# Graph attention of one Trainium2 core: the edge terms built feature by edge instead of edge by feature, and the scores summed in PSUM

## The reference

```python
for i in range(3):
    gl = (h @ Wl[i] + bl[i]).reshape(n, 4, 32)
    gr = (h @ Wr[i] + br[i]).reshape(n, 4, 32)
    xj = gl[src]                                  # a row per edge
    e = xj + gr[dst] + (edge_attr @ We[i])        # edge x 4 heads x 32
    e = leaky_relu(e, 0.2)
    alpha = einsum('ehc,hc->eh', e, att_w[i])     # 4 scores of an edge
    alpha = exp(alpha - segment_max(alpha, dst)[dst])
    alpha = alpha / (segment_sum(alpha, dst)[dst] + 1e-16)
    h = segment_sum(xj * alpha[..., None], dst) + bias[i]
    h = leaky_relu(batch_norm(h, gamma[i], beta[i]), 0.02)
out = h @ Wf + bf
```

## Time and profile before

| | |
|---|---|
| time, median of 3 | 6846.17 us (6832.88 to 6849.38) |
| the profiled execution's time | 6835.19 us |
| its span | 6833.4 us |
| busy: PE, DVE, ACT, POOL | 5228.6, 4419.9, 2485.9, 4656.5 us |
| attention, first gather to last | 3469.4 to 4485.0, 4586.5 to 5601.8, 5705.4 to 6724.0 us |

### The profile page before, as it was taken

The page is one execution under the profiler, slowest core; times in us unless marked ns, Lnnn a source line. Parts: engine busy times, 40 slices in busy tenths (PEclk is TensorE's granted clock), DMA queues, the critical chain, the costliest instruction groups (busy, mean ns, idle before and its releaser), DMA issues.

```text
span 6833.4 us, 117887 instructions
## 1 busy us (share of the span) xinstructions
PE 5228.6 (77%) x33433; PEld 4525.5 (66%) x33433; DVE 4419.9 (65%) x15206; ACT 2485.9 (36%) x9471; POOL 4656.5 (68%) x4868
## 2 busy tenths in 40 slices
PE   8988851888888788788667777767777776777776
PEld 7555541777777677777556666656666665666675
DVE  5434330777676788877757777765766774777776
ACT  2554420777776587777501111110111111111112
POOL 1777776777776477777357777737777764777772
PEclk9999985999999899999879999978999997989887
DMA  2111111544444355544134444434444443444442
GB/s 65 41 39 39 42 24 57 131 126 126 126 126 112 94 151 151 147 142 142 52 108 136 140 135 132 138 79 129 136 140 133 131 121 93 136 135 135 132 132 68
DMA packets 496381, 755.03 MB, mean 110 GB/s; under 512 B 226141, under 2 KB 358593, under 8 KB 494709
## 3 DMA queue, kind: packets, MB, share of 16 engines
q1 hardware_dynamic: 314500, 425.53, 19.9%
q0 software_dynamic: 180928, 315.57, 19.4%
q10 hardware_dynamic: 320, 6.40, 0.4%
HBM read 647.92 MB, written 98.34 MB: 109 GB/s over the span
## 4 chain that ended last, share of the span: by engine, by line
POOL 20%; PE 15%; DVE 13%; issue 11%; DMA 4%; DVEq 2%; ACT 1%; POOLq 0%; ACTq 0%
POOL AR L577 13%; POOL AR L569 7%; PE PS L1342 5%; DVE AR L1938 4%; PE PS L1358 4%; PE PS L1355 3%; DMA AR<-gtab_d,AR 3%; DVE AR L2007 2%; DVE AR L2018 1%; DVEq L505 1%; DMA AR<-ptab_d,AR 1%; PE PS L1256 1%; PE PS L1232 1%; PE PS L1253 1%; DVE AR L2028 1%
## 5 line engine op out<-in xcount | busy, mean ns | idle before, releaser
L577 POOL DMA_INDIRECT AR<-gtab_d,AR x2436 | 2310.8, 949 | 848.2 <-issue 702.1
L569 POOL DMA_INDIRECT AR<-ptab_d,AR x1624 | 1546.7, 952 | 529.1 <-issue 476.7
L1358 PE MATMUL PS<-AR,ident 128*128 128x140 f32 x4872 | 1115.5, 313 | 246.2 <-DMA AR<-gtab_d,AR 243.0
L1342 PE MATMUL PS<-AR 128*112 128x132 f32 x4872 | 895.5, 318 | 395.8 <-DVE AR L1938 368.7
L1355 PE MATMUL PS<-AR 128*128 x4872 | 1093.5, 309 | 68.1 <-issue 67.9
L1342 PEld LDWEIGHTS PS<-AR 128*112 128x112 f32 x4872 | 704.3, 200 | 542.2 <-DVE AR L1938 259.0
L1358 PEld LDWEIGHTS PS<-AR,ident 128*128 128x128 f32 x4872 | 846.8, 212 | 311.2 <-DMA AR<-gtab_d,AR 309.5
L551 POOL DMA_INDIRECT rec_d<-AR x782 | 771.3, 986 | 371.0 <-issue 235.3
L1023 ACT ACTIVATE AR<-AR 128x448 f32<-128x448 bf16 x609 | 335.3, 570 | 1776.2 <-PE PS L1342 1598.5
L2018 DVE SCALAR_TENSOR_TENSOR AR<-PS,AR 128x280 f32<-128x280 f32 x1218 | 536.9, 445 | 674.9 <-PE PS L1358 672.6
L1256 PE MATMUL PS<-AR,ident 128*128 128x160 f32 x3248 | 790.3, 325 | 223.1 <-DMA AR<-ptab_d,AR 218.3
(11 more groups left out here) (347 smaller groups left out, 7417.4 us busy)
## 6 DMA issues: line engine op xcount, KB each, us to landing
AR<-ste_d SPq DMA_DIRECT2D x404, 512.0 KB
AR<-nbb_d SPq DMA_DIRECT2D x303, 224.0 KB
ste_d<-AR SPq DMA_DIRECT2D x101, 512.0 KB
AR<-gtab_d,AR POOLq DMA_INDIRECT x2436
AR<-ptab_d,AR POOLq DMA_INDIRECT x1624
nbb_d<-AR SPq DMA_DIRECT2D x101, 224.0 KB, 2.4
AR<-key_d SPq DMA_DIRECT2D x94, 224.0 KB
AR<-rec_d SPq DMA_DIRECT2D x812, 8.0 KB
```

Of the source, the lines that this page charges most:

```text
L569: e.indirect_dma_start(out=XJ1[:, t % 32, :], out_offset=None, in_=tabs_d[0][:, :], in_offset=off).then_inc(done_, 16)
L577: e.indirect_dma_start(out=xj2(t)[:, t % 4, :], out_offset=None, in_=tabs_d[1][:, :], in_offset=off).then_inc(done_, 16)
L1342: x = e.matmul(PS[6 + v_ % 2][0:B, (t % 2) * 132:(t % 2 + 1) * 132], SQ4[:, i % 4, t % 4, :], PX[:, i % 5, t % 4, :, :].rearrange("p h c - ...
L1358: x = e.matmul(o, ident[:, :], xj2(t)[:, t % 4, :], start=False, stop=True, skip_group_check=True)
```

## The change

The edge terms of a tile are built turned over. PE transposes the gathered rows (`e.transpose`, 128 columns) into PSUM and adds the product of the right table's block with `STE`, so that features lie along the partitions and edges along the columns. ACT copies each tile's block of the right table into a fixed place first (`expander`, a ring `EX` of 12), since it is now the stationary operand of the product. A quad fills one PSUM bank (128 x 512). ACT takes it out with the bias (`LE`), DVE does the leaky ReLU on it within SBUF (`leaked`), and PE makes the scores: a product with a window of `ATW`, a matrix that holds the attention vectors, the window shifted by one column for every tile, so that all tiles of a chunk accumulate in one bank, already in the form that the scans want. The extra columns of the left table, `terms`, `scores`, `AL` and its turning are gone. A row of the table is 132 wide instead of 140 (`GW`), features are kept in another order, the right table is taken out of PSUM by ACT instead of DVE (`gat_out`), with two banks in turn for each table instead of four shared ones, and the products that made the extra columns of the weights are gone.

The rounds change too: chunks of eight quads up to quad 184 (before up to 152), then four of 6, 5, 4 and 4 quads, 27 in all instead of 29 (`NCH`), a chunk's steps in successive rounds throughout (before two rounds apart in 17 chunks), and one quad weighted in each round, 12 rounds after its own (before two in every second round, with 17 to 9 rounds between). The ring `XJ` is 32 quads long instead of 29. `LASTR` is 217 instead of 214.

```diff
-HW = 35
+HW = 33
 GW = 4 * HW
-NXJ = 29
+NXJ = 32
@@ rounds_of_attention
-    ends = list(range(8, 153, 8)) + list(range(157, 198, 5)) + [NQ]
+    ends = list(range(8, 185, 8)) + [190, 195, 199, NQ]
...
-        gap = 2 if c < 17 else 1
-        turn = end + gap
+        turn = end + 1
...
-        back = max(turn + 2 * gap + 1 + gap, px[-1] + 1 if px else 0)
-        steps.append((turn, turn + gap, turn + 2 * gap, turn + 2 * gap + gap - 1, back))
-        for i in range(start, end):
-            r = max(back + 2 - gap, px[-1] if px else 0)
-            while px.count(r) >= 2:
-                r += 1
-            px.append(r)
+        back = max(turn + 3, px[-1] + 1 if px else 0)
+        steps.append((turn, turn + 1, turn + 2, turn + 2, back))
+        px += [back + i for i in range(end - start)]
@@ scalar_program
+            def gat_out(l, b):
+                w.wait_ge(s_mm, mm_at(f"gat{l}", b))
+                done(e.activation(TABG[0:B, b, :], PS[6 + b % 2][0:B, 0:128], ACT.Copy), s_aev)
...
+                for j in range(-2, LASTR):
+                    if j + 2 < NQ:
+                        i = j + 2
+                        if i >= 3:
+                            w.wait_ge(s_e, pair_at(l, 2 * (i - 3) + 1))
+                        for t in range(4 * i, 4 * i + 4):
+                            x = e.activation(expander(t), TABG[:, bass.ds(block_of(cx, "scalar", t), 1), :].rearrange("p a f -> p (a f)"), ACT.Copy)
+                        done(x, s_ex)
...
+                    if 0 <= j < NQ:
+                        w.wait_ge(s_e, pair_at(l, 2 * j + 1))
+                        if j >= 2:
+                            w.wait_ge(s_lin, quad_at(l, j - 2))
+                        done(e.activation(LE[:, j % 2, :], PS[j % 2][:, :], ACT.Identity, bias=BRC[:, l % 2:l % 2 + 1]), s_le)
...
-                for g in range(7):
-                    done(e.activation(XT[:, g * TG:(g + 1) * TG], XT[:, g * TG:(g + 1) * TG], ACT.Identity,
-                                      scale=ST[:, 18:19], bias=ST[:, 19:20]), s_aff)
+                for g in range(9):
+                    if g < 7:
+                        done(e.activation(XT[:, g * TG:(g + 1) * TG], XT[:, g * TG:(g + 1) * TG], ACT.Identity,
+                                          scale=ST[:, 18:19], bias=ST[:, 19:20]), s_aff)
+                    if l < 2 and g >= 2:
+                        for b in range(4 * g - 8, 4 * g - 4):
+                            gat_out(l + 1, b)
@@ tensor_program
-                    w.wait_ge(s_dev, dev_at(p, b - 4, 1))
-                    e.matmul(PS[4 + b % 4][0:B, 0:GW], XT[:, b * B:(b + 1) * B], WLx, start=True, stop=True, skip_group_check=True)
-                    done(e.matmul(PS[4 + b % 4][0:B, GW:2 * GW], XT[:, b * B:(b + 1) * B], WRx, start=True, stop=True, skip_group_check=True), s_mm)
...
+                    w.wait_ge(s_dev, dev_at(p, b - 2))
+                    w.wait_ge(s_aev, aev_at(p, b - 2))
+                    e.matmul(PS[4 + b % 2][0:B, 0:128], XT[:, b * B:(b + 1) * B], WLx, start=True, stop=True, skip_group_check=True)
+                    done(e.matmul(PS[6 + b % 2][0:B, 0:128], XT[:, b * B:(b + 1) * B], WRx, start=True, stop=True, skip_group_check=True), s_mm)
...
-                        if u >= 4:
-                            w.wait_ge(s_att, pair_at(l, u - 4))
...
+                        if u % 2 == 0 and u >= 4:
+                            w.wait_ge(s_le, quad_at(l, u // 2 - 2))
+                        w.wait_ge(s_ex, quad_at(l, u // 2))
                         for t in (2 * u, 2 * u + 1):
-                            o = PS[u % 4][:, (t % 2) * GW:(t % 2 + 1) * GW]
+                            o = PS[(u // 2) % 2][:, (t % 4) * 128:(t % 4 + 1) * 128]
+                            w.wait_ge(*gath_sem(l + 2, t))
+                            e.transpose(o, xj2(t)[:, t % 4, 0:128], ident[:, :])
                             w.wait_ge(*ste_sem(l + 2, t))
-                            e.matmul(o, STE[:, ste_slot(l + 2, t), (t % 8) * 128:(t % 8 + 1) * 128],
-                                     TABG[:, bass.ds(block_of(cp, "tensor", t), 1), :], start=True, stop=False, skip_group_check=True)
-                            w.wait_ge(*gath_sem(l + 2, t))
-                            x = e.matmul(o, ident[:, :], xj2(t)[:, t % 4, :], start=False, stop=True, skip_group_check=True)
+                            x = e.matmul(o, expander(t), STE[:, ste_slot(l + 2, t), (t % 8) * 128:(t % 8 + 1) * 128],
+                                         start=False, stop=True, skip_group_check=True)
                         done(x, s_e)
...
+                    def scores(i):
+                        c = chunk_of(i)
+                        w.wait_ge(s_att, quad_at(l, i))
+                        w.wait_ge(s_arg, chunk_at(l, c - 2))
+                        for kk in range(4):
+                            t = 4 * (i - chunk_start(c)) + kk
+                            x = e.matmul(PS[2 + c % 2][:, 0:128], ATW[:, 31 - t:159 - t], LE[:, i % 2, kk * 128:(kk + 1) * 128],
+                                         start=(t == 0), stop=(i == ENDS[c] - 1 and kk == 3), skip_group_check=True)
+                        done(x, s_lin)
...
+                    if 1 <= j <= NQ:
+                        scores(j - 1)
@@ vector_program
-                    done(e.tensor_tensor(ZG[:, b, :], PS[4 + b % 4][0:B, 0:GW], BLb, ALU.add), s_dev)
-                    done(e.tensor_tensor(TABG[0:B, b, :], PS[4 + b % 4][0:B, GW:2 * GW], BRb, ALU.add), s_dev)
+                    done(e.tensor_tensor(ZG[:, b, 0:128], PS[4 + b % 2][0:B, 0:128], BLb[:, 0:128], ALU.add), s_dev)
...
-                def terms(u):
...
-                    done(e.scalar_tensor_tensor(
-                        AB[:, j % 2, kk:kk + 2, :], PS[u % 4][:, 0:2 * GW].rearrange("p (k f) -> p k f", k=2), 0.0,
-                        attB.unsqueeze(1).to_broadcast([128, 2, GW]), ALU.max, ALU.mult), s_att)
-                def scores(j):
...
-                    done(e.tensor_reduce(AL[:, c % 2, :, t0:t0 + 4].rearrange("p h t -> p t h"),
-                                         AB[:, j % 2, :, :].rearrange("p k (h c) -> p k h c", h=4), AX.X, ALU.add), s_lin)
+                def leaked(j):
+                    w.wait_ge(s_le, quad_at(l, j))
+                    done(e.scalar_tensor_tensor(LE[:, j % 2, :], LE[:, j % 2, :], 0.2, LE[:, j % 2, :], ALU.mult, ALU.max), s_att)
...
                     if j < NQ:
-                        terms(2 * j)
-                        add()
-                        terms(2 * j + 1)
-                        add()
-                        scores(j)
-                        add()
-                    if len(quads) > 1:
-                        add()
-                        weight(quads[1])
+                        leaked(j)
                     while tiles:
                         add()
```

More of the change, by code:

```diff
@@ L488, in groups_up_to @@
             return sum(1 for _, lo, _ in SG if load_of(lo) <= i)
-        ENG = {"vector": mybir.EngineType.DVE, "tensor": mybir.EngineType.PE}
+        ENG = {"vector": mybir.EngineType.DVE, "tensor": mybir.EngineType.PE, "scalar": mybir.EngineType.Activation}
         def record_tile(cache, t):
@@ L556, in gpsimd_program @@
                 w.wait_ge(s_dve, DV[("henc", "h0_3", "h1_3", "ov0_6", "ov1_6")[layer]])
-                mile(e.memset(acc_flat, 0.0), f"acc{layer}")
+                mile(e.memset(acc_flat if layer < 2 else acc2, 0.0), f"acc{layer}")
                 if layer < 2:
@@ L2062, in vector_program @@
                     quads = weighted_in(j)
+                    add()
+                    if quads:
+                        weight(quads[0])
+                    add()
                     for n, step in ((0, scans), (1, carries), (2, args)):
@@ L2155, in arrange @@
     h = lambda n: i["L1_gnn_" + n]
+    by_head = np.arange(128).reshape(4, 32).T.reshape(-1)
+    inner = lambda x: c(x[..., by_head])
+    layers = lambda x: c(np.stack([x[0], x[1][by_head], x[2][by_head]])[..., by_head])
     return {
```

171 lines of the change are left out of this document (72 added, 99 removed).

## The result

The changed kernel takes 6876.37 us (median of 5, 6867.27 to 6887.12) against 6846.17 (median of 5, 6832.88 to 6850.21): a ratio of 1.005, with a 95% interval of 1.0033 to 1.0067. The profiled executions have spans of 6874.2 and 6833.4 us, 40.8 apart.

What follows compares the result with a forecast made beforehand. POOL's issue of attention gathers was taken as the bound. Terms +60 (`leaked`), -1 (chunk steps), -52 (tails), -3 (ahead of layer one), +1 (projections) make +5 on 6846.17: 6851, stated as 6852, range 6791 to 6930.

Steps and rivals of the forecast that it cites:

- A: Attention layers: POOL stays the bound and `leaked` meets some gathers; 6814 to 6904 us, chance 0.52.
- POOL is the bound and stays it: Attention layers: POOL's gathers, 1.25 us apart, wait for nobody between a layer's first and last; 3 x 1015 us.
- `leaked` lengthens the gathers that start under it, by what is left of it less 0.13 us: Attention gathers: `leaked`, both inputs in SBUF, delays a gather's end by its remaining time less 0.13 us, 609 occurrences.
- The size of that term: Gathers lengthened by `leaked`: 0.121 us each at random phase, 74 us in all; 60 booked, bounds 0 and 300.
- a fixed part of the phases: Gathers meeting `leaked`: some phases always harmless, so 60 us taken instead of 74.
- The tails: Last gather to normalising step in each layer: 46 us instead of 62.6, 63.7 and 66.8; -52 us booked.
- in the tail a round costs what DVE and PE need: Rounds after a layer's last gathers: 3 x 0.45 + 0.82 = 2.2 us each, without `pair` and `leaked`; 40 us taken.
- case D: Tails don't shorten because PE and DVE wait for one another's answers: +57 us, 6903, chance 0.08.
- The loop under 5.0 us: PE, ACT and DVE loop per round: 4.1 us at full clock, 6.4 at half, mean 4.5, below POOL's 5.0.
- The lower price for the transpose: PE's transpose in the attention rounds: 0.11 to 0.22 us, between half a product and a whole one.
- Projections and the start of layer one: Projections +1 us over three layers from two banks; -3 us ahead of layer one, extra-column products gone.
- Case B: Attention layers: `leaked` locks into a harmless place behind a gather's start; -55 us, 6791, chance 0.25.

Runs made afterwards that it cites:

- e3: Kernel before plus, per quad ahead of the weighting, a product of gathered rows with themselves, both inputs in SBUF: 8803.13 us against 8492.64 on a slow chip.
- e4: Kernel before with the weighting done twice, one input in SBUF and one in PSUM: 8822.79 us against 8492.64 on a slow chip.
- e9: Changed kernel with the leaky ReLU's maximum taken from PSUM, one input in SBUF: 6789.83 us against 6842.49 of the kernel before, ratio 0.9926.
- e10: Changed kernel with the maximum from PSUM and a layer's last 19 quads weighted two in a round: 6791.11 us, 0.992 of the kernel before.

## Why the prediction was right, point by point

It said 6852 with a range of 6791 to 6930; measured were 6876.37. The signs of the terms and the case were right (A, own range 6814 to 6904), the point 24 us too low. Between the two profiles the sum was +5 and came out as +40.8: of the 35.8 between, 14.6 lie in the layers, 13.4 in the tails, 6.9 in the first part, mostly the one long transfer. That `leaked` was the price and the tails the gain was no luck; but the two large terms nearly cancel, both were set too favourably, and the range, 139 us wide, held either sign.

- **POOL is the bound and stays it**: shown. Idle time before the gathers is 848.2 and 848.9 us; of it 702.1 and 733.9 are issue, 107 in each the wait of a layer's first gather for its table, and only 22.6 and 5.8 are ended by PE. Two gathers stand 0.30 us apart by the timelines; the prediction's 0.29 would not quite give its 1.25.
- **`leaked` lengthens the gathers that start under it, by what is left of it less 0.13 us**: shown three ways, by 270 meetings in the changed kernel (71.5 us measured, 72.4 by the sum), by e3 against e4, and by e9, which takes the second input from PSUM and gets 75.4 us back. The Trainium skill (SBUF — State Buffer, "Who interferes with whom") says that a VectorE instruction with at most one SBUF input does not contend with GpSimd. The trace of e9 agrees: with one input in PSUM the excess is -0.1 us over 272 meetings. The other half of the rule that the prediction cites, that whoever starts first holds the port for the whole instruction, isn't seen where the gather starts first: 430 L2031 began under a running gather and lasted 0.67 to 0.70 us, as elsewhere.
- **The size of that term**: booked 60, measured 71.5 by the meetings and 75 by e9. The plain sum for a random phase had given 74; I took it down to 60 for "a fixed part of the phases" that would be harmless. Here the phase is nearly random: `leaked` starts are spread over the whole 1.25 us between gathers, 25 to 96 in each tenth of a microsecond up to 1.2. With the 0.69 us that it lasts the plain sum gives 76, so at most 5 us were saved by the phase, and the discount of 14 had no ground.
- **The tails**: booked -52, measured -38.6. The step that was mis-sized is "in the tail a round costs what DVE and PE need" with its 2.2 us, and the 40 us for the rounds made from it (16 quads "at 2.2 to 2.6"). The parts ahead of it were right in the changed kernel's layer one: the last transpose 4.3 us behind the gather, the last `leaked` done 2.0 us later; then the rounds take 44.7 us and not 40. The sum left the waits out, even the 0.47 us for a scattering that stands in its own row at 4538.15. The changed kernel's tail, with the granted clock (third figure from a row's end) of the whole and of one stretch in it:

```profile
4521.00:4567.00 46.00, 32.10 (x149) 27.07 (x149) 27.88 (x92) 7.75 (x17) 0.00 (x0) 0.64 0.25 73
4539.00:4545.00 6.00, 4.96 (x22) 4.32 (x20) 3.84 (x12) 2.00 (x4) 0.00 (x0) 0.50 0.35 99
...
4529.60 0.70 DVE L2023 TENSOR_TENSOR AR<-AR,PS 128x528 f32<-128x528 f32 x1
...
4535.80 0.29 DVE L1954 TENSOR_TENSOR AR<-AR,PS 112x132 f32 x1 [2.97 <-PE PS L1367]
4536.01 0.70 DVE L2023 TENSOR_TENSOR AR<-AR,PS 128x528 f32<-128x528 f32 x1
...
4539.45 0.29 DVE L1954 TENSOR_TENSOR AR<-AR,PS 112x132 f32 x1 [0.97 <-PE PS L1367]
4539.66 0.70 DVE L2023 TENSOR_TENSOR AR<-AR,PS 128x528 f32<-128x528 f32 x1
4540.27 0.28 DVE L1954 TENSOR_TENSOR AR<-AR,PS 112x132 f32 x1
4540.78 0.29 DVE L1954 TENSOR_TENSOR AR<-AR,PS 112x132 f32 x1 [0.22 <-DVE AR L1954]
4541.22 0.29 DVE L1954 TENSOR_TENSOR AR<-AR,PS 112x132 f32 x1 [0.15 <-DVE AR L1954]
4542.05 0.29 DVE L1954 TENSOR_TENSOR AR<-AR,PS 112x132 f32 x1 [0.53 <-PE PS L1367]
```

  From one `weight` (L2023) to the next is a round. The shortest, from 4539.66 to 4542.26, last 2.60 us: four adds, and DVE waits 0.53 us for the last one's scattering. The round from 4529.60 to 4536.01 lasts 6.41 us: it holds a chunk's carries on DVE, after which PE still has two small products and a quad's scattering to do while DVE waits 2.97 us. From 4523.23 to 4561.31 eleven rounds take 38.1 us, 3.5 us each. That is the waiting for one another that the prediction had as case D, in part and not enough to keep the tails at 63 us. The clock isn't what the sum had wrong: the earlier trace rows stand at the half clock as well (granted clock 0.50 for 4534 to 4539), and a round of five adds without a wait for PE lasts 2.79 us at the full clock (4523.23 to 4526.02) and at the half one (4542.26 to 4545.05). How the 5 us a layer divide among the waits isn't worked out. 51.0, 51.5 and 52.0 us were measured where 46 were forecast. Whether the lighter round of DVE or the new table made the tails shorter than before stays open: the runs on it met only slow chips. The rows of the last gather reach PE as forecast (4 us; 4.3, 4.5 and 4.8 measured).
- **The loop under 5.0 us**: right, as far as POOL never waits for it; doubling PE's terms of 0.3, 0.5 and 1.3 would give 6.2 and not 6.4 at the half clock, which changes nothing here. The lower price for the transpose holds (transpose to product 0.11 us at the full clock). ACT's eviction takes 687 ns and not 578, which costs nothing.
- **Projections and the start of layer one**: booked +1 and -3; measured +1.1 (1.4 - 0.3) and -2.2.
- **Case B** (a fixed harmless phase) is seen on a slow chip, where the change is 0.35% faster, but not for the prediction's reason: there POOL is not the bound and stands idle in most rounds. In the three traces in which it never waits (the changed kernel's, and the versions with the maximum from PSUM in e9 and e10) no fixed place is found; that a waiting POOL is what fixes it isn't tested.

## What to carry to other kernels

Where GpSimd's indirect gathers set the pace, count the VectorE operations that have both inputs in SBUF: one of length d, at a random phase in a period p between gathers, costs (d - 0.13) squared over 2p, and with one input in PSUM it cost nothing here. The same change is 0.5% slower than the kernel before with two SBUF inputs and 0.7% faster with one. Take a round's price over a whole round, waits included, and not from the distance of two operations in it: that gave 2.2 us where the rounds took 3.5 on the mean. Work taken out of a tail has gone somewhere; see whether the rounds that take it up still fit under the bound.

## What the runs showed that I had not expected

The granted clock in the middle of an attention layer rose from 0.90 to 0.96 with the change (0.97 in e9), with PE busy for 76% of the stretch instead of 78%. No run here shows why.

Chips differ: the kernel before takes 6842 to 6846 us on some and 8493 to 8555 on others, with the same lengths on DVE, ACT and POOL. Between the changed kernel's traces on the two kinds, pauses of all engines at once make up 263 of 1644 us; most of the difference isn't explained. Which of two kernels is the faster changed with it: 1.005 and 0.9965 for the same pair.

Between two VectorE operations that stand back to back a gather seldom gets in if the second begins 0.03 to 0.12 us after the gather's start (10 of 62 did), and mostly if it begins later (10 of 11).

Near a common start it is decided within some 0.05 us who is held. In the changed kernel eight gathers began up to 0.04 us after an L2031 and were not lengthened at all, while the L2031 lasted 0.72 to 0.76 us instead of 0.69; the next, at 0.05 us, was lengthened by 0.51 us.
